# Second attention of a two-layer network: order of the exponentials, place of RoPE's cosine product, and batches in which the experts' results are added

## The reference, cut to what matters

```python
proj = x @ W_in.T + b_in
q, k, v = ...                       # [b, 16, 512, 64] each
q = _rope(q, sin, cos)              # y_lo = x_lo*cos + x_hi*sin
k = _rope(k, sin, cos)              # y_hi = x_hi*cos - x_lo*sin
att = jnp.einsum('bhqd,bhkd->bhqk', q, k) * scale
att = jnp.where(mask, att, -inf)    # causal
att = jax.nn.softmax(att, axis=-1)
y = jnp.einsum('bhqk,bhkd->bhqd', att, v)
return y @ W_out.T + b_out          # x is a layernorm; the result is added to the rows
```

## Time and profile before

| | |
|---|---|
| median of 3 runs | 2377.34 us (2376.03 to 2378.91) |
| profiled execution, device time | 2375.09 us |
| its span, first to last instruction | 2373.3 us |
| busy: PE, DVE, ACT, POOL | 1902.8, 1687.7, 1247.2, 960.1 us |
| first and last row maxima of the second attention | 986.51 us, 2038.13 us |

### The profile page before, as it was taken

How to read it: one execution, slowest core, us unless ns; L and a number is a source line. 1 busy time by engine, 2 the same in 40 slices (tenths; PEclk the granted TensorE clock), 3 DMA queues, 4 the chain that set the end, 5 groups by cost and what they waited for, 6 DMA issues and landing times. The chain is left out here.

```text
span 2373.3 us, 50684 instructions
## 1 busy us (share of the span) xinstructions
PE 1902.8 (80%) x17990; PEld 1282.3 (54%) x17991; DVE 1687.7 (71%) x3654; ACT 1247.2 (53%) x2545; POOL 960.1 (40%) x1103
## 2 busy tenths in 40 slices
PE   2989989899826994667879787888879788539999
PEld 1666666666623663344646455555656465426665
DVE  4888888888762444377776777776777776679997
ACT  1666666666642443456555565656555566234443
POOL 4434553433041001678445454645445455042222
PEclk9999999999758997788989898999999899769999
DMA  7000000000142222223111111111111111100000
GB/s 235 2 1 2 2 2 2 2 2 2 38 173 82 81 84 57 50 48 65 31 33 37 28 37 28 37 28 37 28 37 37 28 37 28 37 1 14 18 15 25
DMA packets 63952, 90.70 MB, mean 38 GB/s; under 512 B 11312, under 2 KB 49360, under 8 KB 63744
## 3 DMA queue, kind: packets, MB, share of 16 engines
q1 hardware_dynamic: 57088, 78.06, 12.1%
q0 software_dynamic: 6656, 9.85, 2.0%
HBM read 35.71 MB, written 18.61 MB: 23 GB/s over the span
## 5 line engine op out<-in xcount | busy, mean ns | idle before, releaser
L880 ACT ACTIVATE prob_sb<-a_bank,neg_max_sb 128x128 f32<-128x128 f32 (+3 forms) x512 | 257.4, 532 | 406.6 <-DVE neg_max_sb L974 406.5
L981 DVE TENSOR_TENSOR p_lo_sb<-a_bank,p_hi_sb 128x384 f16<-128x384 f32 (+1 forms) x384 | 229.8, 598 | 244.0 <-ACT p_hi_sb L889 244.0
L458 DVE TENSOR_REDUCE neg_max_sb<-a_bank 128x1 f32<-128x128 f32 (+3 forms) x512 | 235.7, 485 | 88.2 <-PE a_bank L238 84.3
L381 ACT ACTIVATE probT_sb<-a_bank 128x512 f32<-128x512 f32 (+1 forms) x384 | 198.7, 526 | 137.8 <-PE a_bank L261 132.9
L1094 POOL TENSOR_TENSOR rope_lo_sb<-rope_sb,rope_hi_sb 128x512 f16<-128x512 f32 x128 | 148.1, 1192 | 265.7 <-ACT rope_hi_sb L917 265.7
L813 PE MATMUL a_bank<-xnT_sb,w_in_sb 128*128 128x512 f16 x768 | 216.1, 425 | 16.9 <-DVE v_buf_sb L1011 15.6
L974 DVE TENSOR_REDUCE neg_max_sb<-a_bank 128x1 f32<-128x128 f32 (+3 forms) x512 | 219.9, 482 | 3.4 <-PE a_bank L761 2.0
L889 ACT ACTIVATE p_hi_sb<-a_bank 128x384 f16<-128x384 f32 (+1 forms) x384 | 205.1, 534 | 11.8 <-PE a_bank L771 11.8
L759 PE MATMUL a_bank<-rope_hi_sb 64*128 64x128 f16 (+3 forms) x512 | 81.8, 314 | 150.5 <-ACT prob_sb L880 149.8
L771 PE MATMUL a_bank<-ident_f_sb,prob_sb 128*128 128x128 f32 x1280 | 185.9, 286 | 2.0 <-DVE p_lo_sb L981 1.8
L771 PEld LDWEIGHTS a_bank<-ident_f_sb,prob_sb 128*128 128x128 f32 x1280 | 160.8, 149 | 38.8 <-issue 11.5
(11 more groups left out here) (267 smaller groups left out, 5248.2 us busy)
## 6 DMA issues: line engine op xcount, KB each, us to landing
t_swapped_sb<-t_buf_sb SPq DMA_DIRECT2D x256, 128.0 KB, 2.3
sorted_rows<-zeros_sb SPq DMA_DIRECT2D x1, 4992.0 KB, 24.3
x_in_sb<-sorted_rows SPq DMA_DIRECT2D x39, 128.0 KB, 2.1
sorted_results<-y_moe_sb SPq DMA_DIRECT2D x39, 128.0 KB, 1.7
x_sb_sb<-L_attn_x SPq DMA_DIRECT2D x8, 512.0 KB, 10.4
w_raw_sb<-L_ffn_gate_bank SPq DMA_DIRECT2D x8, 512.0 KB, 3.9
w_raw_sb<-L_ffn_up_bank SPq DMA_DIRECT2D x8, 512.0 KB, 4.8
w_raw_sb<-L_ffn_down_bank SPq DMA_DIRECT2D x8, 512.0 KB, 6.3
```

Source lines behind the costliest of these rows:

```text
L381: act.activation(probT[:, (h // 4) % 2, h % 4, T_AT[r]:T_AT[r + 1]], ST[(3 * h + r) % 2][:, 0:T_AT[r + 1] - T_AT[r]], ACT.Exp).then_inc(s_ ...
L458: last = dve.tensor_reduce(neg_max[:, h % 2, i:i + 1], S[(3 * h + g) % 2][:, off:off + L], AX.X, ALU.max, negate=True)
L880: last = act.activation(prob_of(h, g, slice(off, off + L)), S[h % 2][:, off:off + L], ACT.Exp, bias=neg_max[:, h % 2, i:i + 1])
L981: dve.tensor_tensor(p_lo[g][:, h % 2, :], PT[h % 2][:, 0:GROUP_COLS[g]], p_hi[g][:, h % 2, :], ALU.subtract).then_inc(s_lo, 1)
```

## The change

ScalarE's slot runs both exponentials of the pair first, then the fills, then both `hi`. The cosine product is no longer taken from PSUM by VectorE: GpSimd makes it from `t_buf` (`times_cos`), in the prologue ahead of each pair's rotation and in the slots as GpSimd's last step, one slot after the fill. So TensorE may fill the bank again after ScalarE's copy, and that copy waits until the cosine product four units (two pairs) earlier is made. The cosine table is no longer divided by the weights' scale, and the copy of the biases scaled by it goes. The work aside now runs in all slots: GpSimd adds 4 tiles in slots 0 and 1, 8 in slots 9 to 16 and 16 in slots 1 to 16 of the second batch, one per slot (before: 4 and then 24, two per slot, in slots 10 to 21), and the root group of 24 tiles becomes one of 8 and one of 16, the latter a batch later.

```diff
--- before.py
+++ after.py
@@ -734,7 +734,7 @@
         prologue()
         for s in range((B - 1) * SLOTS_ + TAIL):
-            if s < SLOTS_ and besides:
+            if besides:
                 besides(eng, 2 * s)
                 besides(eng, 2 * s + 1)
@@ -812,7 +812,7 @@
-                taken[bank] = (s_u, unit(b, t, p) + 1)
+                taken[bank] = (s_t, unit(b, t, p) + 1)
@@ -901,8 +901,9 @@
                 wait(act, s_fill, n)
                 U = unit(b, t, p)
                 wait(act, s_sw[U // 2 % 2], 16 * 4 * (U // 4))
+                wait(act, s_u, U - 3)
                 act.activation(t_buf[:, U // 2 % 2, t, :], W[bank][:, :], ACT.Identity, scale=1.0 / W1_SCALE,
-                               bias=w["bias_qk"][:, 0, t * PAIRS + p:t * PAIRS + p + 1]).then_inc(s_t, 1)
+                               bias=w["bias_qk"][:, t * PAIRS + p:t * PAIRS + p + 1]).then_inc(s_t, 1)
@@ -944,13 +945,13 @@
         def slot(parts):
             for b, kind, *c in fills(parts, 1, 1):
                 take(kind, b, *c)
-            for a in range(2):
-                for b, p, g in groups(parts, 0):
+            for b, p, g in groups(parts, 0):
+                for a in range(2):
                     exp(b, 2 * p + a, g)
-                if a == 0:
-                    for b, kind, *c in fills(parts, 0, 0):
-                        take(kind, b, *c)
-                for b, p, g in groups(parts, LAG_HI):
+            for b, kind, *c in fills(parts, 0, 0):
+                take(kind, b, *c)
+            for b, p, g in groups(parts, LAG_HI):
+                for a in range(2):
                     hi(b, 2 * p + a, g)
@@ -995,15 +996,7 @@
         def take(kind, b, *a):
             bank, n = work_banks.next()
-            if kind == "qk":
-                t, p = a
-                U = unit(b, t, p)
-                wait(dve, s_t, U + 1)
-                wait(dve, s_zl, U - 2 * RING + 1)
-                dve.scalar_tensor_tensor(out=rope[:, U % (2 * RING), :], in0=W[bank][:, :],
-                                         scalar=w["bias_qk"][:, 1, t * PAIRS + p:t * PAIRS + p + 1],
-                                         in1=w["cos"][:, t, :], op0=ALU.add, op1=ALU.mult).then_inc(s_u, 1)
-            elif kind == "V":
+            if kind == "V":
@@ -1077,14 +1070,18 @@
     def _(pool):
+        def times_cos(b, t, p):
+            U = unit(b, t, p)
+            wait(pool, s_t, U + 1)
+            pool.tensor_tensor(rope[:, U % (2 * RING), :], t_buf[:, U // 2 % 2, t, :], w["cos"][:, t, :], ALU.mult).then_inc(s_u, 1)
@@ -1105,6 +1102,8 @@
             for p in range(RING):
+                for t in range(2):
+                    times_cos(0, t, p)
                 for t in range(2):
                     rotate(0, t, p)
@@ -1122,6 +1121,8 @@
                     if t_ == t:
                         rotate(b, t, p)
+            for b, kind, t, p in fills(parts, 1, None, "qk"):
+                times_cos(b, t, p)
@@ -1220,7 +1221,7 @@
-    GROUP_A, GROUP_B, GROUP_C = (0, 0, QT), (1, QT, 2 * QT), (2, 2 * QT, N_TILES)
+    GROUP_A, GROUP_B, GROUP_C, GROUP_D = (0, 0, QT), (1, QT, 2 * QT), (2, 2 * QT, 4 * QT), (3, 4 * QT, N_TILES)
@@ -1243,8 +1244,6 @@
-            pool.wait_ge(l1.s_load, 16 * l1.loads)
-            pool.tensor_scalar(l1.bias_qk[:, 1, :], l1.bias_qk[:, 0, :], W1_SCALE, 1.0, ALU.mult, ALU.mult).then_inc(s_scaled, 1)
@@ -1254,13 +1253,13 @@
         if k == GROUPS - 1:
             roots(act, GROUP_C)
+        if k == 2 * GROUPS - 1:
+            roots(act, GROUP_D)
@@ -1268,18 +1267,26 @@
-        if k >= 26 and k % 4 == 2:
-            partial_stats(dve, 2 + (k - 26) // 4)
+        if k in (34, 40):
+            partial_stats(dve, 2 + (k - 34) // 6)
         if k == GROUPS - 2:
             variances(dve, GROUP_C)
         if k == GROUPS - 1:
             invert(dve, GROUP_C)
+        if k - GROUPS in (14, 22, 30, 38):
+            partial_stats(dve, 4 + (k - GROUPS - 14) // 8)
+        if k == 2 * GROUPS - 2:
+            variances(dve, GROUP_D)
+        if k == 2 * GROUPS - 1:
+            invert(dve, GROUP_D)
     def pool_aside(pool, k):
-        if AT_B <= k < AT_B + QT:
-            add_results(pool, QT + k - AT_B)
-        if 20 <= k < 20 + N_TILES - 2 * QT:
-            add_results(pool, 2 * QT + k - 20)
+        if k < QT:
+            add_results(pool, QT + k)
+        if 18 <= k < 18 + 4 * QT and k % 2 == 0:
+            add_results(pool, 2 * QT + (k - 18) // 2)
+        if 2 <= k - GROUPS < 2 + 8 * QT and k % 2 == 0:
+            add_results(pool, 4 * QT + (k - GROUPS - 2) // 2)
@@ -2248,7 +2255,7 @@
-    c["cos"] = np.stack([rows(cc, 0.125 / W1_SCALE), rows(cc, 1.0 / W1_SCALE)])
+    c["cos"] = np.stack([rows(cc, 0.125), rows(cc, 1.0)])
```

More of the change, by code:

```diff
@@ L1079, in _ @@
     def _(pool):
+        def times_cos(b, t, p):
+            U = unit(b, t, p)
+            wait(pool, s_t, U + 1)
+            pool.tensor_tensor(rope[:, U % (2 * RING), :], t_buf[:, U // 2 % 2, t, :], w["cos"][:, t, :], ALU.mult).then_inc(s_u, 1)
         def rotate(b, t, p):
             U = unit(b, t, p)
-            R = U // 2 % 2
+            R, U6 = U // 2 % 2, U % (2 * RING)
             wait(pool, s_sw[R], 16 * 4 * (U // 4 + 1))
@@ L1086, in rotate @@
             wait(pool, s_w, U + 1)
-            U6 = U % (2 * RING)
             pool.tensor_tensor(rope[:, U6, :], rope[:, U6, :], t_sw[:, R, t, :], ALU.add).then_inc(s_z, 1)
@@ L1145, in __init__ @@
         self.bias = self.sb("bias1", [P, HEADS * DH1], F32)
-        self.bias_qk = self.sb("bias_qk1", [P, 2, HEADS], F32)
+        self.bias_qk = self.sb("bias_qk1", [P, HEADS], F32)
         self.bias_out = self.sb("bias_out1", [P, D], F32)
@@ L1168, in load_rest @@
             rest = [(self.bias_out[:, :], d["L1_attn_b_out"].unsqueeze(0).to_broadcast([P, D])),
-                    (self.bias_qk[:, 0, :], d["b_qk1"])]
+                    (self.bias_qk[:, :], d["b_qk1"])]
         if part > 1:
@@ L1255, in l1_attention @@
     raw_scope.close()
-    AT_B = 0
     def act_aside(act, k):
```

## The result

The changed kernel takes 2364.81 us (median of 10 runs, 2359.61 to 2372.43) beside 2377.51 for the kernel before (10 runs): ratio 0.995, 95% interval 0.9934 to 0.9966. That is -12.7 us, small but clear. The forecast was +2. The profiled execution has a span of 2361.3 us against 2373.3: -12.0.

A forecast was written before the change was run, and what follows sets the result against it. Bound in most slots: a loop of VectorE and ScalarE, TensorE beside it. Prologue +4.9, batch 0 -5.3, batch 1 +8.7, batches 2 to 6 -6.0, batch 7 -0.3: +2.0 on 2377.34, so 2379 us, range 2353 to 2406.

The forecast's parts named there:

- the three kinds of slots: Plain slots (0 to 2, 15 to 23): kind 0 gains 0.04 us, kind 1 0.17, kind 2 loses 0.07; batch -0.6.
- slots 3 to 9 and 12 to 14: Middle slots of a batch: earlier exponentials and matmuls give -1.4 us in 3 to 9, -0.9 in 12 to 14.
- the price of slot 10: Slot 10: VectorE's normalize runs into GpSimd's add and both cosines and is blocked; +1.5 us a batch.
- slot 13 clear of the meeting: Slot 13: last cosine ends about 1.1 us before normalize, so GpSimd does not block it; taken as free.
- the prologue: Prologue: GpSimd is the chain; cosines of pairs 1 and 2 stand in it, 4 x 1.22 = +4.9 us.
- A: Slot 10: cosines done before normalize, or only one or two operations wait; up to 2.9 us a batch, 2359; chance 0.20.
- B: Scores' wait for exponentials is the path; 149.8 us come back in large part, about 2230; chance 0.03.
- C: Slot 13: normalize collides with GpSimd there too; 3.5 us in seven batches, 25 us, 2404; chance 0.15.
- D: Batch 1: GpSimd with adds and cosines becomes the bound; about 0.7 us in 16 slots, +11, 2390; chance 0.12.
- Batch 0: First batch: loses 16 adds, 4 sets of statistics (-5.2) and 1.1 of aggregation, against slot 10's +1; -5.3 us.
- Batch 1: Second batch: -1.2 steady, +5.2 statistics, +2.7 aggregation, +2 collisions of adds and normalize; +8.7 us.
- Batch 7: Last batch: no normalize and later no cosine; -0.3 us.

The follow-up runs named there:

- `adds_only`: Kernel before with only the adding of the experts' results and its statistics spread over two batches; ratio 1.0007 to the kernel before.
- `cos_adds`: Changed kernel with ScalarE's slot in the old order (cosine on GpSimd, adds in two batches); ratio 1.0018 to the kernel before.
- `prologue_dve`: Changed kernel with the prologue's six cosine products back on VectorE; ratio 0.9935 to the kernel before.
- `cos_only`: Kernel before with only the cosine product moved to GpSimd; old ScalarE order, adds as before; ratio 1.0023 to the kernel before.
- `order_cos`: Changed kernel with the adds as before (new ScalarE order, cosine on GpSimd); ratio 0.9990 to the kernel before.
- `order_only`: Kernel before with only ScalarE's slot in the new order; cosine on VectorE, adds as before; ratio 1.0143 to the kernel before.
- `norm_early_before`: Kernel before with only the next batch's normalization of tiles 0 to 2 placed behind the row maxima of slots 8, 9, 11; ratio 0.9733.
- `stats_late`: Changed kernel with early normalization (slots 8, 9, 11), prologue cosines on VectorE, statistics behind the row maxima; 2302.5 us, ratio 0.9673 to the kernel before.
- `norm_early`: Changed kernel with normalization of the first three tiles moved behind the row maxima of slots 8, 9, 11; ratio 0.9714 to the kernel before.

## Why the prediction was wrong
**Right.** The bound (a loop of VectorE and ScalarE, not the scores' wait), the three kinds of slots to 0.05 us, slots 3 to 9 and 12 to 14, the price of slot 10 (+1.4 for +1.5), slot 13 clear of the meeting, the steady batches (-5.4 for -6.0), the prologue (+4.7 for +4.9). Rivals A, B and C did not come: slot 10 took 9.70 to 9.73 in all steady batches, batches stayed near 132, slot 13 got shorter. Only in batch 0 did A's "one or two operations wait" come (below). D did not come in batch 1, which grew by 3.0.

**Batch 0, -5.3 forecast, -10.6 measured.** The step that failed priced this batch by three terms alone, -5.2 and -1.1 for statistics and aggregation and +1 for slot 10. The gains of the slots without a meeting, which the sum gives to every steady batch (-0.6, -1.4, -0.9), are left out without a reason; with them the term would have been -8.2. (1) Slots 0 to 5 gave -3.3, of which nothing was in the sum. In these slots there is no output projection of an earlier batch (and no `lo` in slot 0), and TensorE was on the path: VectorE's second maxima waited 0.69 for its scores at 990.54, and the scores 3.80 for an exponential. That wait was in the trace and not looked at. The runs part the -3.3 (length of slots 0 to 5, mean granted clock in them):

| | cosine on VectorE | on GpSimd, old order | on GpSimd, new order |
|---|---|---|---|
| clock 0.83 to 0.86 | 27.08 (before), 27.08 (`adds_only`) | 26.60 (`cos_adds`) | 24.75 (`prologue_dve`) |
| clock 0.93 | | 25.58 (`cos_only`) | 23.74 (changed kernel, `order_cos`) |

So 0.5 is the cosine, 1.8 the order at either clock, and 1.0 the clock (0.84 before, 0.93 after). Here the order does pay, as rival B said of the whole, but only with the cosine gone: `order_only` takes 27.17. (2) Slots 9 to 11 gave -1.5 where +1 stood. In slot 10 (8.74 to 8.76) the meeting cost less than in a steady batch: only two of four operations waited (1.29, 1.37), the fourth ran beside an indirect add in 0.43. Slot 11 was long before already, since one operation waited there for an add and the three operations that GpSimd had behind it; first VectorE, then the last two of the three:
```profile
1050.58 4.38 DVE L1031 TENSOR_SCALAR xn_sb<-x_sb_sb,mv_sb,rstd_sb 128x256 f32<-128x256 f32 x1
...
1051.96 2.84 POOL L1094 TENSOR_TENSOR rope_lo_sb<-rope_sb,rope_hi_sb 128x512 f16<-128x512 f32 x2
```
It fell from 9.88 to 8.56, and to 8.53 in `adds_only`, which has one add a slot there instead of two. (3) Slots 12 to 23 gave -5.7. The statistics and the aggregation, 6.3 in the sum, are not all of it: `adds_only`, which takes out the same, has -3.7 there.

**Batch 1, +8.7 forecast, +3.0 measured.** Against a steady batch of its own kernel it is 6.4 longer, forecast 9.9: the terms of 5.2 for statistics and 2 for meetings were too large. The slots that end with a set (6, 10, 14, 18) are longer by 0.5, 0.3, 0.3 and 1.3, so that only the last of the four has its full price; the aggregation (slots 22 and 23) took 2.4 for 2.7; slots 8, 11 and 13, where adds and normalizations meet, +0.6, -0.9 and +0.8. The other 1.0 is slot 0, of which nothing was in the sum. An indirect add can leave a normalization alone, as in slot 10 of batch 1 after:
```profile
1182.99 1.55 POOL L1195 DMA_INDIRECT x_sb_sb<-sorted_results,pos_sb  x1 [0.15 <-issue]
...
1183.15 0.42 DVE L1032 TENSOR_TENSOR x_sb_sb<-x_sb_sb,bias_out_sb 128x256 f32<-128x256 f32 x1
```
The other 2 us of the error are on the side of before, whose batch 1 was longer than its steady ones by that much: slots 15 and 16 by 1.2, slot 13 by 0.6, slots 0 and 1 by 0.35. The clock was lower in slot 15, where TensorE was busy throughout. Here is that slot of before in batch 1 and in batch 2. The third line is slot 0 of batch 1 of the changed kernel, which had the same there (4.90 in its batch 2):
```profile
1217.51:1223.40 5.89, 5.89 (x46) 3.33 (x45) 3.60 (x10) 3.12 (x7) 5.61 (x5) 0.79 0.02 4
...
1351.85:1356.78 4.93, 4.93 (x48) 2.88 (x46) 3.60 (x9) 2.90 (x7) 4.64 (x5) 1.00 0.00 0
```
```profile
1119.49:1125.41 5.92, 5.92 (x45) 3.63 (x44) 3.21 (x8) 3.12 (x7) 5.63 (x5) 0.75 0.16 22
```
Slot 13 has no such sign (7.77 at 0.87, and 7.18 at 0.75 in batch 2). The sum took before's batch 1 for a steady one, though its length is in the trace.

**Batch 7, -0.3 forecast, -2.1 measured.** Slot 13 fell from 6.19 to 4.66, though it has no `normalize`. That slot before and after:
```profile
1995.43:2001.62 6.19, 6.19 (x59) 3.81 (x57) 3.64 (x10) 2.53 (x5) 2.04 (x2) 0.78 0.30 70
```
```profile
1984.17:1988.83 4.66, 3.86 (x53) 2.44 (x51) 2.98 (x10) 2.39 (x5) 4.52 (x4) 1.00 0.25 56
```
TensorE was busy for the whole of it at a mean clock of 0.78; after, the clock is 1.00 and TensorE idle for 0.8. `norm_early_before`, with the old order and the old cosine, has 1.00 and 4.84 there: at the full clock the old code is 0.2 behind, which is what kind 1 was priced at. The sum took a slot of this shape to cost the same in every batch.

**The parts don't add.** The sum treated the adds as a term of their own (-5.2, +5.2). By the eight combinations their worth is +0.0007 alone, +0.0017 with the order, -0.0005 with the cosine and -0.004 with both; only the last is clear of the intervals. The prediction weighed the load of GpSimd in batch 1 after the change, not what batch 0 would have been without the third part.

The sign was missed by three errors of 1.8, 5.3 and 5.7 us, all in the batches that are unlike the steady one and all in one direction. Part of them goes with the clock: 1.0 (slots 0 to 5 of batch 0), 1.2 (slots 15 and 16 of batch 1) and 1.4 (slot 13 of batch 7) on the side of before, 1.0 (slot 0 of batch 1) on that of the changed kernel, so some 2.6 of 12.8. No term of the sum was for the clock.

**Open.** Why the clock falls in some stretches of one kernel and not in others with nearly the same work; so whether those 2.6 us belong to the change; what lengthens slot 13 of batch 1 before. A version of `stats_late` whose batch 1 has its adds away from slots 8 to 11 was not tried; slots 8 and 11 there take 8.94 and 11.88 against 4.93 and 6.81, some 9 us.

## What to carry to other kernels
Find the loop of waits that closes a slot, then ask of each operation whether it lies in a wait of that loop or between its steps: here taking out a hidden one gave 0.14 of 0.66 us a slot, laying it bare cost 34 us of the kernel. Price the first and the last rounds from their own rows, since other waits end last there. And an edit that moves work to an engine may need a second one that thins that engine's queue: measure them together and apart.

## What the runs showed that was not expected
- A VectorE operation on SBUF beside GpSimd waits not always for one instruction. In `stats_late` (above) it took 4.84 us for 0.43, in slot 11 of the kernel before 4.38, in slot 10 of batch 0 of `cos_adds` 2.78, which is why that slot takes 11.53. In all three it started while an indirect add ran and GpSimd's next tensor operation began 0.3 to 0.6 us later, and it waited until the operations that followed without a gap were done. Where that next operation was 0.8 us or more away it took 0.29 to 0.70. What holds it up in between is not shown.
- A stretch with the lower clock can be worth more than the edit: two plain slots of `cos_only` take 9.37 us at 1.00 and 10.76 at 0.88, and its steady batches 131.5 and 134.6.
- An operation can be blocked and still be well placed: in `norm_early` slot 11's normalization is blocked three times and the slot still 2.7 us shorter, since it begins in a wait.
